# Eight batches of four places in the 32 rows of a column group, instead of four blocks of eight batches, in a two-layer recurrence

## The chip, the cores and the metric

The kernel runs on one core of one Trainium2 chip. The metric is the device time of one execution, in microseconds. Before the change the median of 3 runs is 2086.43 us (2085.79 to 2086.91).

## The reference

Two residual layers, each a plain tanh recurrence over 1024 positions, with 8 batches and 512 features, all in float32:

```python
# x: (8, 1024, 512), cond: (8, 512); Wx, Wh: (512, 512), b: (512,) of each layer
def layer(x, h0, Wx, Wh, b):
    xW = einsum('ntd,dh->tnh', x, Wx) + b
    def step(h, xw_t):
        h_next = tanh(h @ Wh + xw_t)
        return h_next, h_next
    _, hs = scan(step, h0, xW)
    return swapaxes(hs, 0, 1)

x = x + layer(x, cond, L0_Wx, L0_Wh, L0_b)
x = x + layer(x, cond, L1_Wx, L1_Wh, L1_b)
```

A step of a layer needs all of the step before it. Layer 1 at position n needs layer 0's output at position n.

## The kernel before, in words

**Interleaving.** Layer 1 runs eight steps behind layer 0 (`LAG`). Slot s does step s of layer 0 and step s - 8 of layer 1, so there are 1032 slots: in the first eight only layer 0 works, in the last eight only layer 1. In between are 1016 slots with two steps each. In the text below, a step of one layer is "a step", and "the other layer" is the one whose step lies before or after it.

**Column groups.** TensorE is used as four column groups of 32 columns. The weights it holds (the stationary operand) are 32 columns of h or x, and the moving operand is a 128x128 piece of Wh or Wx. Group g produces 32 rows of PSUM (partitions 32g to 32g+31) that hold features 128g to 128g+127 of the output. A k tile is one fourth of the 512 features that are summed over; for it, h has 32 columns of float32 next to each other, and these 32 columns become the 32 rows of every group. Eight batches fill only 8 of the 32 columns. The other 24 are three more *places* for the same eight batches.

**What the places hold.** Before the change, place t of a tile is the block of columns 8t to 8t+7. For the projection x @ Wx, the four places are four successive positions, so that one pass over Wx serves four steps. For step n of the recurrence, the h of step n is put into place (n+1) % 4. For the k tiles 2 and 3 the other places stay zero, and they are multiplied as float32 (`recur_whole`, line 236). For the k tiles 0 and 1, h is cut into bfloat16 parts: the first part is the upper half of h itself, the second is the upper half of h minus the first part, and the third the upper half of what remains then. The second and third part go to two neighbouring places (table `BLOCKS`), and the weights are also in three bfloat16 parts (`recur_parts`, line 253: 2 tiles x 3 parts x 4 groups = 24 matmuls). The rows of PSUM at three neighbouring places then hold terms of one sum, and the fourth place holds nothing.

**One step on the engines.** ACT first writes the projection of the step into the PSUM bank, with the rows of the other positions set to zero by a mask (`begin`, line 339). TensorE adds `recur_whole` and `recur_parts`. Then:

1. `turn` (DVE, line 418) transposes the 128x128 of PSUM in 32x32 blocks into `zt` in SBUF. In it, the 32 columns of a tile k are what the 32 rows were.
2. `total` (DVE, line 424) adds three places of `zt` (from `LOWEST[n % 4]` on) into `z`: 96 elements of each partition become 32.
3. `tanh` (ACT, line 344) writes 32 elements into the place of h.
4. `rest_first` (DVE, line 432) subtracts from h (tiles 0 and 1, 16 elements) its upper half and writes the difference to the next place; `rest_second` (same line) does it once more.
5. `sum_mid` (line 458) or `sum_out` (line 468) adds h to x, 32 elements, on DVE.

**Order.** Every engine works its queue in program order; there is no planner. On TensorE (`slot`, line 272) each slot is: parts of layer 0, a tile of projection, whole of layer 1, parts of layer 1, a tile of projection, whole of layer 0's next step. `recur_whole` waits for `tanh` of the step before, `recur_parts` for its `rest_second`. On DVE (`slot`, line 481) a slot is: `turn(0)`, `rest_second(1)`, `total(0)`, the sums, `rest_first(0)`, `turn(1)`, `rest_second(0)`, `total(1)`, `rest_first(1)`. So `turn` of one layer stands in the queue behind `rest_first` of the other, and ahead of its `rest_second`. `rest_first` waits for the `tanh` of its step, `total` for its `turn`, `tanh` for its `total`. x is loaded and the result stored by four positions at a time (64 KB), on SP's queue.

**What the change touches.** `window` (149), `h_of` (156), `h_cols` (165), `x_of` (171), `total` (420), `rest` (429), the masks (line 506) and the order of x in DRAM. `turn`, `project`, `recur_whole` and `recur_parts` are untouched: each reads 32 columns of a tile.

Of the kernel before, what the change touches and what calls it, by code (L numbers as in the profile page):

```python
# [12 lines left out]
P = 128  # L13
B, T, D = 8, 1024, 512
KC = D // P
KB = (2, 2)
PARTS = 3
QG = 4
S4 = 4
ROWS = S4 * B  # L20
COLS = KC * B
GRP = S4 * COLS
# [4 lines left out]
HALF = 4 * (P + B)  # L27
# [9 lines left out]
def number(l, s):  # L37
    n = s - LAG * l
    return n if 0 <= n < T else None
# [6 lines left out]
PROJECT = (((0, 1), (0, 2)), ((0, 3), (1, 0)), ((1, 1), (1, 2)), ((1, 3), (0, 0)))  # L46


BLOCKS = ((0, 1, 2), (1, 0, 2), (2, 1, 3), (3, 1, 2))
LOWEST = (0, 0, 1, 1)  # L50


def build(nc, x, h_init, weights, out):
    ctx = ExitStack()
    with ctx:
        def sb(name, shape, dt=F32):
            return ctx.enter_context(nc.sbuf_tensor(name, shape, dt))
# [4 lines left out]
        def sem(name):  # L62
            return ctx.enter_context(nc.semaphore(name))
# [11 lines left out]
        ones = sb("ones", [P, P])  # L75
# [5 lines left out]
        zt = [[sb(f"zt{l}_{i}", [P, P]) for i in range(2)] for l in LAYERS]  # L81
# [15 lines left out]
        s_ones = sem("ones_made")  # L97
# [32 lines left out]
        def h_count(l, n):  # L130

            s = n + LAG * l
            steps = [(m, t) for t in range(s - s % S4, s + 1) for m in LAYERS if counted(m, t)]
            return h_done[s // S4 % 2], steps.index((l, s)) + 1

        def is_split(l, n):

            return (n >= -S4 if l else n >= PARTED - 1) and n < T - 1

        def split_count(l, n):  # L140

            s = n + LAG * l
            return split_done[l][s // S4 % 2], s % S4 + 1
# [3 lines left out]
        def window(n):  # L147

            w = n % RING
            return w // 4 * HALF + w % 4 * P + (32 if w % 4 == 3 else 0), B * ((n + 1) % 4)  # L150

        def h_step(l, n):
            at, _ = window(n)
            return h[l][:, at:at + P].rearrange("p (k r) -> p k r", r=ROWS)

        def h_of(l, n):
            off = window(n)[1]
            return h_step(l, n)[:, :, off:off + B]

        def h_bits(l, n):  # L160

            at, _ = window(n)
            return h[l][:, at:at + P].bitcast(BF16).rearrange("p (k r two) -> p k r two", r=ROWS, two=2)[:, :, :, 1]

        def h_cols(n, part):


            at = BLOCKS[(n + 1) % S4][part] * B
            return slice(at, at + B)

        def x_of(xs, n):
            return xs[n // S4 % 2][:, :].rearrange("p (k s b) -> p s k b", s=S4, b=B)[:, n % S4]

        @block.sync
        def _(sp):
# [152 lines left out]
        def _(act):  # L328
# [13 lines left out]
            def tanh(l, n):  # L342
                act.wait_ge(z_done[l], n + 1)  # L343
                act.activation(h_of(l, n), z[l][n % 2][:, :].rearrange("p (k b) -> p k b", k=KC), ACT.Tanh).then_inc(  # L344
                    h_count(l, n)[0], 1)
# [68 lines left out]
        @block.vector  # L414
        def _(dve):
            def turn(l, n):
                dve.wait_ge(rec_done, STEP_AT[l, n])  # L417
                dve.transpose(zt[l][n % 2][:, :], ps_rec[l][n % 2][:, 0:P]).then_inc(zt_done[l], 1)  # L418

            def total(l, n):  # L420

                at = LOWEST[n % S4] * B
                dve.wait_ge(zt_done[l], n + 1)
                dve.tensor_reduce(z[l][n % 2][:, :].rearrange("p (k b) -> p k b", k=KC),  # L424
                                  zt[l][n % 2][:, :].rearrange("p (k r) -> p k r", r=ROWS)[
                                      :, :, at:at + PARTS * B].rearrange("p k (i b) -> p k b i", b=B),
                                  AX.X, ALU.add).then_inc(z_done[l], 1)

            def rest(l, n, part):

                step, to, of, tiles = h_step(l, n), h_cols(n, part), h_cols(n, part - 1), slice(0, KB[l])
                return dve.tensor_tensor(step[:, tiles, to], step[:, tiles, of], h_bits(l, n)[:, tiles, of],  # L432
                                         ALU.subtract)

            def rest_first(l, n):
                if is_split(l, n):
                    dve.wait_ge(*h_count(l, n))
                    rest(l, n, 1).then_inc(rest_done[l], 1)

            def rest_second(l, n):  # L440
                if is_split(l, n):
                    dve.wait_ge(rest_done[l], n + 1 if l else n + 2 - PARTED)
                    rest(l, n, 2).then_inc(split_count(l, n)[0], S4 if (l, n) == (0, PARTED - 1) else 1)

            def lower(l, n):

                if (n + LAG * l) % S4 == 0 and is_split(l, n - 1):
                    done, count = split_count(l, n - 1)
                    dve.sem_inc(done, -count)

            def sum_mid(n):

                c, t = n // S4, n % S4
                if n >= 2 * S4:
                    dve.wait_ge(out_done, n - 2 * S4 + 1)
                if n == T - 1:
                    dve.wait_ge(*h_count(0, n))
                add = dve.tensor_tensor(x_of(x_mid, n), x_of(x_dve, n), h_of(0, n), ALU.add)  # L458
                if t == S4 - 1:
                    add.then_inc(mid_done, 1)  # L460

            def sum_out(n):
                c, t = n // S4, n % S4
                if t == 0 and c >= 2:
                    dve.wait_ge(out_free[c % 2], DMA * (c // 2))
                if n == T - 1:
                    dve.wait_ge(*h_count(1, n))
                dve.tensor_tensor(x_of(x_out, n), x_of(x_mid, n), h_of(1, n), ALU.add).then_inc(out_done, 1)  # L468

            def sums(s):  # L470

                c = (s + S4 - 1) // S4
                if s % S4 == 0 and c < NG:
                    dve.wait_ge(x_dve_loaded[c % 2], DMA * (c // 2 + 1))
                if (n := number(1, s - 1)) is not None:
                    sum_out(n)
                if (n := number(0, s - 1)) is not None:
                    sum_mid(n)

            def slot(s):  # L480

                n0, n1, before = number(0, s), number(1, s), number(1, s - 1)
                if n0 is not None:
                    turn(0, n0)
                if before is not None:
                    rest_second(1, before)
                if n0 is not None:
                    lower(0, n0)
                    total(0, n0)
                sums(s)  # L490
                if n0 is not None:
                    rest_first(0, n0)
                if n1 is not None:
                    turn(1, n1)
                if n0 is not None:
                    rest_second(0, n0)
                if n1 is not None:
                    lower(1, n1)
                    total(1, n1)
                    rest_first(1, n1)  # L500

            dve.memset(zeros[:, :], 0.0).then_inc(s_zeros, 1)
            dve.memset(h[0][:, :], 0.0).then_inc(s_clear, 1)
            dve.memset(ones[:, :], 0.0).then_inc(s_ones, 1)
            dve.wait_ge(s_ones, 1)
            for t in range(S4):
                at = (ROWS + B) * t
                dve.memset(ones[:, at:at + B], 1.0).then_inc(s_ones, 1)
            dve.wait_ge(s_ones, 1 + S4)
            dve.transpose(mask[:, :], ones[:, :]).then_inc(s_mask, 1)  # L510
            dve.wait_ge(s_clear, 2)
            dve.wait_ge(s_first, DMA)
            for dst in (h_of(0, -1), h_of(1, -1)):
                dve.tensor_copy(dst, h_first[:, :].rearrange("p (k b) -> p k b", k=KC)).then_inc(s_hinit, 1)  # L514
            dve.wait_ge(s_hinit, 2)
            rest(1, -1, 1).then_inc(s_hrest, 1)
            dve.wait_ge(s_hrest, 1)
            rest(1, -1, 2).then_inc(split_count(1, -1)[0], S4)
            for s in range(T + LAG + 1):
                slot(s)  # L520
# [28 lines left out]
```

## Time and profile before

| | |
|---|---|
| median of 3 runs | 2086.43 us |
| the profiled execution | 2085.73 us |
| its span | 2083.9 us |
| granted TensorE clock | 1.00 of full |
| busy, share of the span | PE 99%, weight loads 86%, DVE 82%, ACT 54%, POOL 1% |
| mean HBM traffic | 26 GB/s |

The profile is of one execution. Busy is the share of the span in which an engine had an instruction under way. Matmuls overlap and their ends are modelled, so the 99% of PE isn't a measure of how much it could still take. Weight loads (PEld) stand apart from the matmuls (PE), with which they overlap. "Idle before" is the time in which the engine had nothing under way before an instruction, with what released it. Instructions on DVE and ACT overlap a little too: one is started while the last one still writes.

### The profile page before, as it was taken

To read this page: it belongs to the slowest core of one execution; us is meant where nothing else is said; L and a number is where in the kernel's file an instruction comes from. 1 tells how busy PE (TensorE), PEld (TensorE's weight loads), DVE (VectorE), ACT (ScalarE), POOL (GpSimd) and SP (SyncE) were. 2 spreads that over 40 slices of the span, in tenths; PEclk is the share of its full clock that TensorE was granted. 3 is DMA by queue.
4 is the path that set the end of the run, shared out by engine and by line. 5 is a ranking of instruction groups with operands and counts; after the bars stand their busy time and mean duration, and the time that the engine had idled before them with its cause. 6 is when DMAs were issued, how large, how long until landed. Compare 5 with 4: busy or idle time off the path is not lost.

```text
span 2083.9 us, 213827 instructions
## 1 busy us (share of the span) xinstructions
PE 2065.8 (99%) x98428; PEld 1792.3 (86%) x98428; DVE 1716.2 (82%) x10234; ACT 1121.8 (54%) x4612; POOL 14.3 (1%) x22
## 2 busy tenths in 40 slices
PE   7999999999999999999999999999999999999998
PEld 6888888888888888888888888888888888888887
DVE  5888888888888888888888888888888888888887
ACT  3555555555555555555555555555555555555554
POOL 2000000000000000000000000000000000000000
PEclk9999999999999999999999999999999999999999
DMA  3000000000000000000000000000000000000000
GB/s 107 23 27 23 27 23 27 23 27 23 27 23 27 23 27 23 27 23 27 23 27 23 27 23 27 23 27 23 27 23 27 23 27 23 27 23 27 23 27 15
DMA packets 112495, 56.00 MB, mean 27 GB/s; under 512 B 12496, under 2 KB 111072, under 8 KB 112096
## 3 DMA queue, kind: packets, MB, share of 16 engines
q1 hardware_dynamic: 111456, 53.53, 9.0%
q14 instruction: 130, 1.06, 0.2%
q10 hardware_dynamic: 864, 1.18, 0.2%
q8 instruction: 13, 0.21, 0.0%
q0 software_dynamic: 32, 0.02, 0.0%
HBM read 37.90 MB, written 16.78 MB: 26 GB/s over the span
## 4 chain that ended last, share of the span: by engine, by line
PE 98%; DVE 0%; DMA 0%; issue 0%; ACT 0%; SPq 0%; DVEq 0%; ACTq 0%
PE ps_rec L236 43%; PE ps_rec L253 34%; PE ps_xw L215 21%; DMA wh<-wh_in 0%; DVE zt L418 0%; DVE z L424 0%; ACT h L344 0%; SPq L181 0%; SPq L183 0%; SPq L179 0%; ACT ps_rec L339 0%; DVE x_out L468 0%; DVEq L417 0%; ACTq L343 0%
## 5 line engine op out<-in xcount | busy, mean ns | idle before, releaser
L236 PE MATMUL ps_rec<-wh,h 128*32 128x128 f32 x32912 | 1256.3, 273 | 11.2 <-ACT h L344 8.4
L253 PE MATMUL ps_rec<-wh_part,h 128*32 128x128 bf16 x48960 | 1058.8, 221 | 2.3 <-issue 2.3
L344 ACT ACTIVATE h<-z 128x32 f32<-128x32 f32 x2048 | 470.2, 230 | 826.0 <-DVE z L424 809.9
L236 PEld LDWEIGHTS ps_rec<-wh,h 128*32 128x32 f32 x32912 | 826.8, 109 | 89.3 <-ACT h L344 13.8
L432 DVE TENSOR_TENSOR h<-h 128x16 f32<-128x16 f32 x4080 | 627.0, 154 | 303.2 <-ACT h L344 302.7
L253 PEld LDWEIGHTS ps_rec<-wh_part,h 128*32 128x32 bf16 x48960 | 705.4, 96 | 193.9 <-issue 2.8
L339 ACT ACTIVATE ps_rec<-ps_xw,mask 128x128 f32<-128x128 f32 x2048 | 670.5, 328 | 119.4 <-PE ps_xw L215 94.8
L418 DVE STREAM_TRANSPOSE zt<-ps_rec 128x128 f32<-128x128 f32 x2048 | 638.8, 312 | 19.9 <-PE ps_rec L236 10.8
L424 DVE TENSOR_REDUCE z<-zt 128x32 f32<-128x96 f32 x2048 | 544.2, 266 | 1.5 <-DVE zt L418 0.9
L215 PE MATMUL ps_xw<-wx,x_pe 128*32 128x128 f32 x8232 | 402.7, 273 | 0.3 <-DMA wx<-wx_in 0.3
L215 PE MATMUL ps_xw<-wx,x_mid 128*32 128x128 f32 x8192 | 401.4, 273 | 0.0
L458 DVE TENSOR_TENSOR x_mid<-x_dve,h 128x32 f32<-128x32 f32 x1024 | 198.1, 193 | 35.1
L468 DVE TENSOR_TENSOR x_out<-x_mid,h 128x32 f32<-128x32 f32 x1024 | 185.4, 181 | 0.3 <-ACT h L344 0.3
L215 PEld LDWEIGHTS ps_xw<-wx,x_pe 128*32 128x32 f32 x8232 | 181.7, 110 | 1.3 <-DMA wx<-wx_in 0.8
L215 PEld LDWEIGHTS ps_xw<-wx,x_mid 128*32 128x32 f32 x8192 | 181.0, 110 | 0.0
L332 ACT ACTIVATE ps_xw<-bias 128x128 f32<-128x128 f32 x514 | 142.0, 277 | 10.2 <-DMA bias<-b_in 2.1
L300 PE MATMUL ps_rec<-zeros 128*32 128x512 bf16 x100 | 8.3, 465 | 0.0
L300 PEld LDWEIGHTS ps_rec<-zeros 128*32 128x32 bf16 x100 | 3.1, 118 | 2.6 <-issue 2.2
L408 POOL TENSOR_TENSOR wh_rest<-wh 128x512 f32<-128x512 f32 x4 | 4.1, 1037 | 6.8 <-DMA wh<-wh_in 6.7
L412 POOL TENSOR_TENSOR wh_part<-wh_rest 128x512 bf16<-128x512 f32 x4 | 4.1, 1036 | 0.0
L514 DVE COPY h<-h_first 128x32 f32<-128x32 f32 x2 | 0.3, 176 | 4.5 <-DMA h_first<-cond_t 4.5
L386 ACT ACT_TABLE_LOAD x1 | 1.3, 1283 | 4.2 <-issue 4.2
(18 smaller groups left out, 11.1 us busy)
## 6 DMA issues: line engine op xcount, KB each, us to landing
x_pe<-x_t SPq DMA_DIRECT2D x256, 64.0 KB, 1.8
x_dve<-x_t SPq DMA_DIRECT2D x256, 64.0 KB, 1.9
out_t<-x_out SPq DMA_DIRECT2D x256, 64.0 KB, 1.5
wh<-wh_in SPq DMA_DIRECT2D x1, 1024.0 KB, 4.7
wx<-wx_in SPq DMA_DIRECT2D x1, 1024.0 KB, 8.1
wx<-wx_in ACTq DMA_DIRECT2D x2, 256.0 KB, 5.5
wx<-wx_in SPq DMA_DIRECT2D x2, 256.0 KB, 5.3
wh<-wh_in SPq DMA_DIRECT2D x2, 256.0 KB, 7.3
```

Of the source, the lines that this page charges most:

```text
L215: mm = pe.matmul(rows(ps_xw[l][c % 2], g), src, wx[l][:, k, g * P:(g + 1) * P], start=False, stop=False, skip_group_check=True, tile_posit ...
L236: mm = pe.matmul(rows(ps_rec[l][n % 2], g), h_step(l, n - 1)[:, k, :], wh[l][:, k, g * P:(g + 1) * P], start=False, stop=k == KC - 1 and n ...
L253: mm = pe.matmul(rows(ps_rec[l][n % 2], g), h_bits(l, n - 1)[:, k, :], wh_part[l][:, i, at:at + P], start=False, stop=k == KB[l] - 1 and i ...
L300: pe.matmul(bank[32 * g:32 * g + 32, :], zeros[:, 0:ROWS], zeros[:, :], start=True, stop=False, skip_group_check=True, tile_position=(0, 3 ...
L332: return act.activation(ps_xw[l][c % 2][:, 0:P], bias[l][:, :], ACT.Copy)
L339: act.activation(ps_rec[l][n % 2][:, 0:P], ps_xw[l][c % 2][:, 0:P], ACT.Copy, scale=mask[:, 32 * t:32 * t + 1]).then_inc(begun[l], 1)
L344: act.activation(h_of(l, n), z[l][n % 2][:, :].rearrange("p (k b) -> p k b", k=KC), ACT.Tanh).then_inc(h_count(l, n)[0], 1)
L418: dve.transpose(zt[l][n % 2][:, :], ps_rec[l][n % 2][:, 0:P]).then_inc(zt_done[l], 1)
L424: dve.tensor_reduce(z[l][n % 2][:, :].rearrange("p (k b) -> p k b", k=KC), zt[l][n % 2][:, :].rearrange("p (k r) -> p k r", r=ROWS)[:, :, ...
L432: return dve.tensor_tensor(step[:, tiles, to], step[:, tiles, of], h_bits(l, n)[:, tiles, of], ALU.subtract)
L458: add = dve.tensor_tensor(x_of(x_mid, n), x_of(x_dve, n), h_of(0, n), ALU.add)
L468: dve.tensor_tensor(x_of(x_out, n), x_of(x_mid, n), h_of(1, n), ALU.add).then_inc(out_done, 1)
```

## The change

The place becomes the inner index of a tile's 32 columns, and the batch the outer one: place t of batch b is column 4b + t instead of 8t + b. The kernel's arithmetic, the number of instructions and their order stay. The addresses change: `total` reads three places that are neighbours in memory, and goes on to the next batch 4 floats further, where it read three elements 8 floats apart. `tanh`, `rest`, `sum_mid` and `sum_out` touch one float in four, where they had runs of eight. x is stored in DRAM with the position innermost, and a load is still one contiguous row of each partition. `BLOCKS` is renamed to `PLACES`.

```diff
-BLOCKS = ((0, 1, 2), (1, 0, 2), (2, 1, 3), (3, 1, 2))
+PLACES = ((0, 1, 2), (1, 0, 2), (2, 1, 3), (3, 1, 2))
 LOWEST = (0, 0, 1, 1)
...
-            return w // 4 * HALF + w % 4 * P + (32 if w % 4 == 3 else 0), B * ((n + 1) % 4)
+            return w // 4 * HALF + w % 4 * P + (32 if w % 4 == 3 else 0), (n + 1) % 4
...
         def h_of(l, n):
-            off = window(n)[1]
-            return h_step(l, n)[:, :, off:off + B]
+            return h_step(l, n).rearrange("p k (b s) -> p k b s", s=S4)[:, :, :, window(n)[1]]
...
-        def h_cols(n, part):
-            at = BLOCKS[(n + 1) % S4][part] * B
-            return slice(at, at + B)
+        def place(ap, n, part):
+            return ap.rearrange("p k (b s) -> p k b s", s=S4)[:, :, :, PLACES[(n + 1) % S4][part]]
 
         def x_of(xs, n):
-            return xs[n // S4 % 2][:, :].rearrange("p (k s b) -> p s k b", s=S4, b=B)[:, n % S4]
+            return xs[n // S4 % 2][:, :].rearrange("p (k b s) -> p s k b", s=S4, b=B)[:, n % S4]
...
             def total(l, n):
-                at = LOWEST[n % S4] * B
+                at = LOWEST[n % S4]
                 dve.wait_ge(zt_done[l], n + 1)
                 dve.tensor_reduce(z[l][n % 2][:, :].rearrange("p (k b) -> p k b", k=KC),
-                                  zt[l][n % 2][:, :].rearrange("p (k r) -> p k r", r=ROWS)[
-                                      :, :, at:at + PARTS * B].rearrange("p k (i b) -> p k b i", b=B),
+                                  zt[l][n % 2][:, :].rearrange("p (k b s) -> p k b s", b=B, s=S4)[
+                                      :, :, :, at:at + PARTS],
                                   AX.X, ALU.add).then_inc(z_done[l], 1)
 
             def rest(l, n, part):
-                step, to, of, tiles = h_step(l, n), h_cols(n, part), h_cols(n, part - 1), slice(0, KB[l])
-                return dve.tensor_tensor(step[:, tiles, to], step[:, tiles, of], h_bits(l, n)[:, tiles, of],
+                step, bits = h_step(l, n)[:, 0:KB[l], :], h_bits(l, n)[:, 0:KB[l], :]
+                return dve.tensor_tensor(place(step, n, part), place(step, n, part - 1), place(bits, n, part - 1),
                                          ALU.subtract)
...
             for t in range(S4):
-                at = (ROWS + B) * t
-                dve.memset(ones[:, at:at + B], 1.0).then_inc(s_ones, 1)
+                dve.memset(ones[:, t * ROWS:(t + 1) * ROWS].rearrange("p (b s) -> p b s", s=S4)[:, :, t],
+                           1.0).then_inc(s_ones, 1)
```

The host code orders x and the result in the same way.

## Rows read from the trace of the kernel before

**Rows 1.** The page: busy time and share of each engine.
```profile
PE 2065.8 (99%) x98428; PEld 1792.3 (86%) x98428; DVE 1716.2 (82%) x10234; ACT 1121.8 (54%) x4612; POOL 14.3 (1%) x22
```

**Rows 2.** Timeline, two steps: start us, us, engine, line, instruction [idle <-releaser].
```profile
1002.15 0.17 DVE L432 TENSOR_TENSOR h<-h 128x16 f32<-128x16 f32 x1
1002.17 0.40 PEld L236 LDWEIGHTS ps_rec<-wh,h 128*32 128x32 f32 x16
1002.23 0.61 PE L236 MATMUL ps_rec<-wh,h 128*32 128x128 f32 x16
1002.25 0.31 DVE L418 STREAM_TRANSPOSE zt<-ps_rec 128x128 f32<-128x128 f32 x1
1002.48 0.13 DVE L432 TENSOR_TENSOR h<-h 128x16 f32<-128x16 f32 x1
1002.59 0.26 DVE L424 TENSOR_REDUCE z<-zt 128x32 f32<-128x96 f32 x1
1002.66 0.34 PEld L253 LDWEIGHTS ps_rec<-wh_part,h 128*32 128x32 bf16 x24
1002.67 0.52 PE L253 MATMUL ps_rec<-wh_part,h 128*32 128x128 bf16 x24
1002.89 0.23 ACT L344 ACTIVATE h<-z 128x32 f32<-128x32 f32 x1 [0.33 <-DVE z L424]
1003.15 0.17 DVE L432 TENSOR_TENSOR h<-h 128x16 f32<-128x16 f32 x1 [0.30 <-ACT h L344]
1003.24 0.31 DVE L418 STREAM_TRANSPOSE zt<-ps_rec 128x128 f32<-128x128 f32 x1
```

**Rows 3.** Timeline, the last eight steps, layer 1 alone.
```profile
2072.48 0.52 PE L253 MATMUL ps_rec<-wh_part,h 128*32 128x128 bf16 x24
2073.04 0.32 DVE L418 STREAM_TRANSPOSE zt<-ps_rec 128x128 f32<-128x128 f32 x1 [0.56 <-PE ps_rec L253]
```

**Rows 4.** Groups by line, 500 to 1500 us: count | busy us, mean ns | idle before.
```profile
L253 PEld LDWEIGHTS ps_rec<-wh_part,h 128*32 128x32 bf16 x23976 | 344.9, 96 | 94.0
L418 DVE STREAM_TRANSPOSE zt<-ps_rec 128x128 f32<-128x128 f32 x1000 | 311.8, 312 | 0.0
L432 DVE TENSOR_TENSOR h<-h 128x16 f32<-128x16 f32 x1999 | 306.9, 154 | 147.7 <-ACT h L344 147.7
L424 DVE TENSOR_REDUCE z<-zt 128x32 f32<-128x96 f32 x999 | 265.7, 266 | 0.4 <-DVE zt L418 0.4
L344 ACT ACTIVATE h<-z 128x32 f32<-128x32 f32 x999 | 229.4, 230 | 391.9 <-DVE z L424 383.9
L215 PEld LDWEIGHTS ps_xw<-wx,x_pe 128*32 128x32 f32 x4000 | 88.0, 110 | 0.0
```

**Rows 5.** Line 253, 1002 to 1003 us: ns min/median/max.
```profile
L253 PE MATMUL ps_rec<-wh_part,h x40: 219/219/228, 1001.8 to 1003.0; 128*32 128x128 bf16 x40
```

**Rows 6.** Lines 432 (one `rest_first`, from 1002.15), 458, 514, 386: ns min/median/max.
```profile
L432 DVE TENSOR_TENSOR h<-h x1: 175/175/175, 1002.2 to 1002.2; 128x16 f32<-128x16 f32 x1
...
L458 DVE TENSOR_TENSOR x_mid<-x_dve,h x499: 191/192/195, 501.5 to 1498.5; 128x32 f32<-128x32 f32 x167
...
L514 DVE COPY h<-h_first x2: 173/176/180, 7.5 to 7.6; 128x32 f32<-128x32 f32 x2
...
L386 ACT ACTIVATE table<-zeros x1: 203/203/203, 5.5 to 5.5; 128x1 f32<-128x1 bf16 x1
```

**Rows 7.** Line 418, whole span: the number of steps.
```profile
L418 DVE STREAM_TRANSPOSE zt<-ps_rec x2048: 306/311/319, 11.2 to 2080.8; 128x128 f32<-128x128 f32 x187
```

More of the change, by code:

```diff
@@ L530 @@
     arrays = {
-        "x_t": packed(x.reshape(B, T // S4, S4, QG, KC, 32).transpose(3, 5, 1, 4, 2, 0).reshape(P, T // S4, GRP)),
+        "x_t": packed(x.reshape(B, T // S4, S4, QG, KC, 32).transpose(3, 5, 1, 4, 0, 2).reshape(P, T // S4, GRP)),
         "cond_t": packed(cond.reshape(B, QG, KC, 32).transpose(1, 3, 2, 0).reshape(P, COLS)),
@@ L547 @@
     return np.ascontiguousarray(
-        got.reshape(QG, 32, T // S4, KC, S4, B).transpose(5, 2, 4, 0, 3, 1).reshape(B, T, D))
+        got.reshape(QG, 32, T // S4, KC, B, S4).transpose(4, 2, 5, 0, 3, 1).reshape(B, T, D))
```

## The prediction

> **What bounds the kernel now.** The page comes first [rows 1]: PE is busy for 99% of the span, weight loads for 86%, DVE for 82%, ACT for 54%. That looks like a TensorE kernel, and the change gives TensorE not one instruction more or less. But PE's ends are modelled, so the next view is the timeline of two steps in the middle [rows 2], read for who starts right after whom. One step takes 1.00 us there (`turn` starts at 1002.25 and 1003.24; 1000 transposes in 1000 us [rows 4]). Every start has a predecessor that it follows as closely as it can, and these close into loops:
>
> - **Loop A, on DVE and ACT.** `turn` starts at 1002.25, `total` 0.34 later (0.31 of transpose and 0.03 of semaphore), `tanh` 0.30 later (0.26 and 0.03 to 0.04), `rest_first` 0.26 later (0.23 and 0.03), and the other layer's `turn`, which stands behind it in DVE's queue, 0.09 later. The sum, 0.99 to 1.00, is the whole period. ACT had been idle when `tanh` began, for `total`, and DVE when `rest_first` began, for `tanh` (147.7 us over 1000 steps [rows 4]); neither is waiting for TensorE.
> - **Loop B, through TensorE.** `turn` 1002.25, `rest_second` of the other layer behind it at 1002.48, the first weight load of that layer's parts at 1002.66 (0.13 of work and 0.05 of semaphore), the matmuls at 1002.67, and the next `turn` at 1003.24, 0.57 after them. This too sums to 1.00.
> - **TensorE itself.** Its loads of the parts come 0.01 us ahead of their matmuls, while those of `recur_whole` come 0.06 ahead [rows 2], and the load engine idles 94 ns a step before the parts and not at all before the projection [rows 4]. The parts' loads are thus late: the first matmuls of the parts take 228 ns instead of 219 [rows 5]. So PE's own need is about 9 ns under the period, some 991 ns.
>
> Is `turn` held by TensorE or by `rest_first`? In the last eight steps DVE is idle before `turn`, and it starts 0.56 us after the parts' matmuls did [rows 3]. In the middle it is 0.57 [rows 2]. So `turn` could start about 0.01 us earlier for all that TensorE holds it back, and loop A is the tightest, with loop B and TensorE within about 10 ns (1%) of it. That is the frame of the forecast: nothing shorter than about 10 ns a step can be won, and every ns added to loop A is paid in full, 2032 times. That number is the 2048 steps [rows 7] less 16, the eight of each layer that run alone.
>
> **The change part by part.** The sum goes by ns a step.
>
> *`total`*, in loop A. It reads 96 elements, now 8 floats apart and then three neighbours. What has the stride cost so far? Started from idle, `rest_first` takes 175 ns for 16 elements and `sum_mid` 192 for 32 [rows 6], which is 1.06 ns an element on 158 ns fixed. By this, 96 elements without any stride cost would take 158 + 102 = 260 ns, and `total` takes 266 [rows 4]. So I take -6. The other end: against the copy, which writes the same 32 elements and reads 32 instead of 96 in 176 ns [rows 6], the 64 more cost 1.41 ns each; if all above half of that were stride, 96 x 0.4 = 37 ns would go. The end on the other side is 0; runs of three that start at an odd float might even cost, but the strided form has no such run to compare, and I leave it at 0.
>
> *`rest_first`*, in loop A by the time it keeps DVE (`turn` starts 0.09 after it), and *`rest_second`*, in loop B by its full length. Both read two operands and write one, all with one float in four; now they have runs of eight. No row shows an operation with scattered writes. The low end is 0. For the high end I let each of the 16 elements cost as much as three contiguous ones: 2 x 16 x 1.06 = +34. I take +17, one more element time for each element: half-way, and a guess, since the nearest row, the contiguous 1.06 ns, says only what such an element costs at least.
>
> The Trainium skill, "Vector Engine (DVE) Microarchitecture Reference", section 5.2, says that a port runs at full rate only while its elements come in pairs of adjacent 4-byte words, and gives 1.05 ns a column for contiguous operands, 1.98 when all three hop at every element and about 2.50 for a small step. Going by it alone, 16 elements would cost 15 to 23 ns more, an estimate from that page; no run here shows it yet.
>
> *`tanh`*, in loop A by its full length. It reads `z` as before, contiguous, and writes one float in four. One element takes 203 ns and 32 take 230 [rows 6, 4], 0.84 ns an element. The low end is 0, the high end one more element time each, 32 x 0.84 = +27. I take +5: only one of its two sides is scattered, and 0.84 ns an element is ACT's reckoning of its own rate, not of the memory's.
>
> *The sums*, with 32 scattered elements on three operands: +34 at the value taken for `rest`. `sum_mid` or `sum_out` ends well before the next `rest_first`, which finds DVE idle for 0.30 us [rows 2]. With the cover of 300 ns they cost nothing. *TensorE*: the same 32 adjacent columns per load, nothing. *Loads and stores*: the same contiguous rows, nothing. *Masks*: four small writes at the start, under 0.1 us.
>
> Loop A: -6 + 17 + 5 = +16 ns. Loop B: -10 of slack, +17 = +7; it stays beneath, and TensorE gets slack. 2032 x 16 ns = +32.5 us. In the eight steps at the end, where one layer is alone, both rests are in the chain: 8 x (34 - 6 + 5) = +0.3 us; in the first eight there are no parts and it is nothing. The profiled execution took 2085.73 us, so 2085.7 + 32.8 = 2118.5; the median of the runs lies 0.7 us above that execution, so **2119 us**, 1.6% slower.
>
> **The rivals.**
>
> - *R1, scattering is free.* 16 or 32 elements are few, and the extra time could hide in the fixed 158 ns. For it: 96 strided reads in `total` show almost no cost. Against it: those are reads of one operand with one write for three reads, while `rest` has two reads and a write for every element. Then only `total` changes, by -6 to -37. Loop A falls by that, and TensorE and loop B stop the gain at about -10. At -6 it is 2086.4 - 12 = 2074, at -10 2066 us.
> - *R2, it cancels, or the period isn't loop A's.* If `total` gives back as much as `rest` and `tanh` take, within 2 ns, or if a step has more room than I read from starts printed to 10 ns, the time stays at 2086.4. Against it: the four intervals of loop A add up to the period with nothing left over.
> - *R3, loop B takes over.* If strides in `total` did cost (-37) and `rest` costs +17, loop A is 1000 - 37 + 17 + 5 = 985, but `rest_second` is in loop B: 1000 - 10 + 17 = 1007. That is 2086.4 + 14 = 2101 us, slower although `total` became much faster. The point from which it decides: as soon as `rest_second` grows by over 10 ns, no gain in `total` can make the kernel faster. The same section of the Trainium skill gives 1.73 ns an element where one source hops at every element, by which `total` would have been paying a good 60 ns for its stride (an estimate from the page); its 266 ns speak against that.
> - *R4, scattering is dear.* `rest` at +34, `tanh` at +10, `total` -5: +39 a step, 2086.4 + 79 + 0.5 = 2166 us.
>
> That the change doesn't do what it says has little room: `total` will read three neighbours, and all other patterns are plain in the diff.
>
> **How the numbers follow.** Forecast 0.42, with its own range 2103 to 2143 (+8 to +28 ns a step); R1 0.23; R2 0.13; R3 0.10; R4 0.12. Faster and slower mean by over 0.2%, about 4 us or 2 ns a step, which is what measurements of this kernel can tell from none. Faster is R1, 0.23; same is R2, 0.13; slower is the rest, 0.64. The range goes from R1's lower end to the cheap side of R4: 2066 to 2152.
>
> **What would show it.** Durations in the changed profile: line 424 at about 260 ns instead of 266; line 432 from 175 to about 192 for `rest_first`, and `rest_second` from 0.13 us to about 0.15; line 344 from 230 to about 235; lines 458 and 468 some 30 ns longer. The distance from `rest_first` to `turn` from 0.09 to 0.11, the period 1.016, and the weight loads of the parts further ahead of their matmuls than 0.01, since TensorE now waits a little. Idle of PE or PEld before line 236 or 253 should appear. I am wrong if `rest` keeps its durations, if `total` falls by more than 10 ns, or if the period doesn't move although loop A's parts do.

## The result

The changed kernel takes 2155.69 us (median of 6 runs, 2154.54 to 2157.03) against 2086.91 us of the kernel before (6 runs beside them): 1.0331 times as long, 95% interval 1.032 to 1.0342. That is 3.3% or 68.8 us slower. Slower was forecast, but 1.6% of it, and the time lies above the range given (2066 to 2152).

The timeline of the changed kernel, two steps from the middle; the lines answer to [rows 2], with line 430 for 432, 416 for 418, 422 for 424 and 342 for 344:

```profile
1001.78 0.19 DVE L430 TENSOR_TENSOR h<-h 128x16 f32<-128x16 f32 x1
1001.89 0.31 DVE L416 STREAM_TRANSPOSE zt<-ps_rec 128x128 f32<-128x128 f32 x1
1002.12 0.15 DVE L430 TENSOR_TENSOR h<-h 128x16 f32<-128x16 f32 x1
1002.23 0.25 DVE L422 TENSOR_REDUCE z<-zt 128x32 f32<-128x96 f32 x1
1002.33 0.34 PEld L251 LDWEIGHTS ps_rec<-wh_part,h 128*32 128x32 bf16 x24
1002.33 0.52 PE L251 MATMUL ps_rec<-wh_part,h 128*32 128x128 bf16 x24
1002.52 0.26 ACT L342 ACTIVATE h<-z 128x32 f32<-128x32 f32 x1 [0.29 <-DVE z L422]
1002.81 0.20 DVE L430 TENSOR_TENSOR h<-h 128x16 f32<-128x16 f32 x1 [0.33 <-ACT h L342]
1002.91 0.31 DVE L416 STREAM_TRANSPOSE zt<-ps_rec 128x128 f32<-128x128 f32 x1
```

The instructions of both loops follow one another as closely as before. `turn` starts at 1001.89 and 1002.91, 1.02 apart in this pair; over the middle it is 967 steps in 1000 us. The groups by line of the same stretch, 500 to 1500 us, against [rows 4 and 6] (count | busy us, mean ns | idle before):

```profile
L430 DVE TENSOR_TENSOR h<-h 128x16 f32<-128x16 f32 x1932 | 331.9, 172 | 159.5 <-ACT h L342 159.5
L416 DVE STREAM_TRANSPOSE zt<-ps_rec 128x128 f32<-128x128 f32 x967 | 298.2, 308 | 0.0
L342 ACT ACTIVATE h<-z 128x32 f32<-128x32 f32 x966 | 255.6, 265 | 400.0 <-DVE z L422 391.7
L422 DVE TENSOR_REDUCE z<-zt 128x32 f32<-128x96 f32 x966 | 244.4, 253 | 0.4 <-issue 0.4
L456 DVE TENSOR_TENSOR x_mid<-x_dve,h 128x32 f32<-128x32 f32 x483 | 109.0, 226 | 16.5
L466 DVE TENSOR_TENSOR x_out<-x_mid,h 128x32 f32<-128x32 f32 x483 | 104.2, 216 | 0.1
```

Means of single durations: `total` won 13 ns (266 to 253), the rests lost 18 (154 to 172), the sums 34 each, and `tanh` 35 (230 to 265). The page of the changed kernel has a warning for whoever reads busy shares. Its first row and the first of its chain of waits, and behind them the chain's row of the kernel before:

```profile
PE 2135.4 (99%) x98428; PEld 1783.4 (83%) x98428; DVE 1751.0 (81%) x10234; ACT 1140.4 (53%) x4612; POOL 14.4 (1%) x22
...
DVE 80%; ACT 13%; issue 5%; PE 2%; DMA 0%; SPq 0%; DVEq 0%; ACTq 0%
```
```profile
PE 98%; DVE 0%; DMA 0%; issue 0%; ACT 0%; SPq 0%; DVEq 0%; ACTq 0%
```

PE is "99% busy" in both, with the same 98428 matmuls, and took 70 us more of it: with matmuls that overlap and ends that are modelled, waiting looks like work. The chain went through PE before and goes through DVE and ACT now.

Of the signs that the prediction named, those on durations are answered above. The idle time of the load engine before the parts rose from 94 to 128 ns a step, but PE shows none, and the parts' loads did not move further ahead of their matmuls: by the starts in the trace they are 3 ns ahead before the change and 2 ns after it. The loads still follow `rest_second` at once: they come 202.5 ns after its start, of which 150 are its own time, and came 185.7 after it with 132 before the change.

The timeline prints hundredths of a us, and a step's sum needs less. So the loops are followed below in means of the distances between starts, in ns, worked out from the starts in the trace between 200 and 1900 us (1640 to 1720 steps for each). Loop A is `turn` to `total` to `tanh` to `rest_first` to the other layer's `turn`; loop B is `turn` to `rest_second` to the first load of the parts to the next `turn`.

```
kernel               period | A: turn-total  -tanh  -rest_first  -turn | B: turn-rest_second  -loads  -turn
before               1000.9 |     346.7      299.2     262.2      92.8 |        236.1         185.7   578.9
after                1035.1 |     343.5      286.7     297.6     107.3 |        232.8         202.5   599.8
e1 total only        1000.4 |     351.4      286.8     262.7      99.6 |        240.5         185.7   574.1
e2 tanh only         1031.4 |     344.1      297.7     297.0      92.5 |        233.1         185.8   612.5
e3 rests only        1020.0 |     350.5      296.2     262.5     110.7 |        239.7         205.2   575.1
e4 sums only         1001.4 |     347.7      296.8     266.8      90.1 |        236.3         186.0   579.1
e5 after, tanh back  1017.7 |     351.0      286.5     266.6     113.7 |        240.2         202.4   575.1
e6 rest_first only   1012.0 |     343.6      298.0     262.6     107.8 |        233.0         185.3   593.6
e7 rest_second only  1018.8 |     351.1      295.4     262.6     109.7 |        240.4         204.0   574.4
e8 pairs             1002.4 |     350.1      289.3     267.5      95.5 |        239.2         187.2   576.0
e11 no rest_second    996.5 |     345.3      296.8     262.1      92.3 |          -             -       -
e12 same, and total   991.5 |     349.8      287.6     262.0      92.1 |          -             -       -
```

Both sums equal the period in every row (to 0.2 ns), since distances around a closed loop always do; that they add up says nothing about which loop decides. Which loop is the tight one is read from two columns: the last of A is 92 to 93 where `turn` only waits for DVE to get done with `rest_first` (107 to 108 where that is scattered), and more where it waits for TensorE; the last of B is 574 to 576 where `turn` waits for TensorE alone, and more where it doesn't.

### The profile page after: what moved, and what is told of

The parts are those of the page before. It is cut to its first block, busy times and chain, and to the rows that moved or that the text cites. A ratio compares the mean times of both kernels' runs of the same rounds, so it can differ in the third digit from the quotient of the medians.

```text
span 2153.3 us, 213827 instructions
## 1 busy us (share of the span) xinstructions
PE 2135.4 (99%) x98428; PEld 1783.4 (83%) x98428; DVE 1751.0 (81%) x10234; ACT 1140.4 (53%) x4612; POOL 14.4 (1%) x22
## 3 DMA queue, kind: packets, MB, share of 16 engines
q14 instruction: 130, 1.06, 0.2%
## 4 chain that ended last, share of the span: by engine, by line
DVE 80%; ACT 13%; issue 5%; PE 2%; DMA 0%; SPq 0%; DVEq 0%; ACTq 0%
DVE h L430 24%; DVE z L422 21%; DVE zt L416 17%; ACT h L342 13%; DVE x_mid L456 11%; DVE x_out L466 7%; PE ps_rec L234 1%; PE ps_rec L251 0%; DMA wh<-wh_in 0%; PE ps_xw L213 0%; SPq L179 0%; SPq L181 0%; SPq L177 0%; ACT ps_rec L337 0%; DVEq L415 0%
## 5 line engine op out<-in xcount | busy, mean ns | idle before, releaser
L342 ACT ACTIVATE h<-z 128x32 f32<-128x32 f32 x2048 | 541.7, 264 | 870.2 <-DVE z L422 852.8
L430 DVE TENSOR_TENSOR h<-h 128x16 f32<-128x16 f32 x4080 | 701.5, 172 | 338.6 <-ACT h L342 338.1
L234 PEld LDWEIGHTS ps_rec<-wh,h 128*32 128x32 f32 x32912 | 817.4, 109 | 99.5 <-ACT h L342 14.1
L416 DVE STREAM_TRANSPOSE zt<-ps_rec 128x128 f32<-128x128 f32 x2048 | 631.8, 309 | 19.5 <-PE ps_rec L234 11.3
L422 DVE TENSOR_REDUCE z<-zt 128x32 f32<-128x96 f32 x2048 | 518.3, 253 | 1.5 <-issue 0.6
L456 DVE TENSOR_TENSOR x_mid<-x_dve,h 128x32 f32<-128x32 f32 x1024 | 232.1, 227 | 34.8
L466 DVE TENSOR_TENSOR x_out<-x_mid,h 128x32 f32<-128x32 f32 x1024 | 220.6, 215 | 0.5 <-ACT h L342 0.3
```

What stands on the lines that cost most here:

```text
L234: mm = pe.matmul(rows(ps_rec[l][n % 2], g), h_step(l, n - 1)[:, k, :], wh[l][:, k, g * P:(g + 1) * P], start=False, stop=k == KC - 1 and n ...
L430: return dve.tensor_tensor(place(step, n, part), place(step, n, part - 1), place(bits, n, part - 1), ALU.subtract)
```

## The experiments

Each part of the change was made alone on the kernel before.

**e1: `total` only.** It adds the wrong places.

```diff
-                at = LOWEST[n % S4] * B
+                at = LOWEST[n % S4]
-                                  zt[...].rearrange("p (k r) -> p k r", r=ROWS)[:, :, at:at + PARTS * B].rearrange("p k (i b) -> p k b i", b=B),
+                                  zt[...].rearrange("p (k b s) -> p k b s", b=B, s=S4)[:, :, :, at:at + PARTS],
```

> The kernel before, with one part of the change alone: total reads three neighbouring floats and goes on by four (it adds the wrong terms; everything else stays in blocks). Theory (two loops): total takes 253 ns instead of 266, as in the changed kernel, so loop A falls from 1001 to about 985 ns a step, but loop B (turn, rest_second, loads of the parts, matmuls) and TensorE stop it at 991 to 996: 2067 to 2077 us. Rival 1 (only loop A counts): -16 ns a step in full, 2054 us. Rival 2 (TensorE alone sets the 1001 ns): no change, 2087 us.

2085.41 us against 2087.65, ratio 0.9989 (0.998 to 0.9999): next to nothing, where the theory had expected 2067 to 2077. `total` did take 253 ns, and its distance in loop A fell by 12. But B's last distance fell only to 574.1 and A's last rose to 99.6: `turn` now waited for TensorE. It also ran longer, as its mean in the groups by line shows (312 in [rows 4]):

```profile
L418 DVE STREAM_TRANSPOSE zt<-ps_rec 128x128 f32<-128x128 f32 x999 | 316.6, 317 | 0.0
L424 DVE TENSOR_REDUCE z<-zt 128x32 f32<-128x96 f32 x1000 | 253.2, 253 | 0.4 <-DVE zt L418 0.4
```

So loop B, when it is the tight one, comes to 1000 ns. It had no 10 ns to spare. This run alone doesn't yet tell loop B from TensorE's own need.

**e2: `tanh` only.** h holds its values in the wrong columns.

```diff
-                act.activation(h_of(l, n), z[l][n % 2]...
+                act.activation(scat(h_step(l, n), (n + 1) % S4), z[l][n % 2]...   # scat: one float in four
```

> The kernel before, with one part of the change alone: tanh writes one float in four (so h holds the values in the wrong columns; nothing else changes). Theory: tanh takes 264 instead of 230 ns and loop A grows by the whole of it, +35 ns a step x 2032 = +71 us, 2158 us, although TensorE and loop B have no more to do. Rival (the 35 ns come only because DVE scatters at the same time, the two getting in each other's way): tanh stays at 230 ns and the time at 2087 us. Rival (part of it was hidden in slack): 2120 us or less.

2147.29 us, ratio 1.0287 (1.027 to 1.0305), a little under the 2158 expected. `tanh` takes 264 ns without any scattered work on DVE, so it isn't contention:

```profile
L348 ACT ACTIVATE h<-z 128x32 f32<-128x32 f32 x970 | 256.5, 264 | 409.1 <-DVE z L428 397.8
L428 DVE TENSOR_REDUCE z<-zt 128x32 f32<-128x96 f32 x970 | 256.2, 264 | 0.5 <-DVE zt L422 0.5
```

The period grew by 30.5 rather than 35: `turn` and `total` are 3 and 1.5 ns quicker to pass on, `turn` because it now starts well after TensorE would let it (more on this at the end).

**e3: both rests only.** The rests work on a tile `hs` of their own, of h's shape.

```diff
-                return dve.tensor_tensor(step[:, tiles, to], step[:, tiles, of], h_bits(l, n)[:, tiles, of], ALU.subtract)
+                return dve.tensor_tensor(scat(step, to), scat(step, of), scat(bits, of), ALU.subtract)
```

> The kernel before, with one part of the change alone: rest_first and rest_second read and write one float in four (of a tile of their own that nobody else reads, so the parts 2 and 3 of h are missing). Theory: 175 to 193 and 131 to 149 ns; loop A grows by 15 to 18 ns a step, loop B by 18 from 10 below the period, so loop A decides: +30 to +37 us, 2117 to 2124 us. Rival (loop B has no slack, both rests are paid): +36 ns, 2160 us. Rival (rests hidden): 2087 us.

2124.22 us, ratio 1.0175 (1.0158 to 1.0192), at the upper end of what was expected, but not for the reason given: the table has A's last distance at 110.7 and B's at 575.1, so loop B decided here, at 1020. It had no 10 ns of slack, as the rival says, but the two rests aren't added up either.

**e4: the sums only.** `x_of` as in the changed kernel, and h from `hs`, a tile of zeros, one float in four.

> The kernel before, with one part of the change alone: sum_mid and sum_out read and write one float in four (h from a tile of its own that stays zero). Theory: both become 34 ns longer (192 to 226, 181 to 215) and the time stays within 0.1% of 2087 us, since DVE is idle for 300 ns behind them. Rival (DVE's total time matters, it is 82% busy): +17 ns a step on average or more, 2120 us.

2086.42 us, ratio 0.9994 (0.9984 to 1.0003): no change, with sums of 224 and 216 ns:

```profile
L471 DVE TENSOR_TENSOR x_mid<-x_dve,hs 128x32 f32<-128x32 f32 x499 | 112.0, 224 | 17.1
L481 DVE TENSOR_TENSOR x_out<-x_mid,hs 128x32 f32<-128x32 f32 x500 | 108.2, 216 | 0.0
```

The reason given doesn't hold, though. The 0.30 us of idle time that the expectation and the prediction count on stand before layer 1's `rest_first`. Both sums stand behind `total` of layer 0 and directly ahead of layer 0's `rest_first`. The last sum and that `rest_first`, in the kernel before (for the second see [rows 2], from 1002.15) and in e4:

```profile
1001.99 0.19 DVE L458 TENSOR_TENSOR x_mid<-x_dve,h 128x32 f32<-128x32 f32 x1
```
```profile
1001.71 0.22 DVE L471 TENSOR_TENSOR x_mid<-x_dve,hs 128x32 f32<-128x32 f32 x1
1001.84 0.17 DVE L445 TENSOR_TENSOR h<-h 128x16 f32<-128x16 f32 x1
```

Between 200 and 1900 us, `rest_first` started 29 ns before the end of `sum_mid` in the kernel before and 87 ns before it in e4. One DVE instruction starts at most 76 to 89 ns before the end of the one ahead in these traces, so the cover was some 60 ns, an estimate from these numbers, and not 300. The two sums added 34 + 34 = 68, and in layer 0 `rest_first` came 271 ns after the start of `tanh` instead of 262. The time doesn't show it: `total` took 263 ns instead of 266 here, `rest_first` of layer 0 only 170 instead of 175, and the mean period is 1001.4 against 1000.9. In the changed kernel the longer `tanh` pays for the cover: `rest_first` starts 60 ns before the end of `sum_mid`, as `tanh` demands. With `tanh` put back (e5) it is 89 ns again, and 271 ns after `tanh`.

**e5: the changed kernel with `tanh` put back.**

```diff
-                act.activation(h_of(l, n), z[l][n % 2]...
+                act.activation(h_step(l, n)[:, :, B * window(n)[1]:B * window(n)[1] + B], z[l][n % 2]...
```

> The changed kernel, with tanh alone put back to runs of eight floats (so h holds its values in the wrong columns). Theory (two loops): tanh 264 -> 230 ns; loop A falls by 35 from 1035 to 1000 ns a step, and now loop B decides, with rest_second at 150 ns: about 240 + 203 + 575 = 1018, so 2120 to 2125 us, half of what the tanh is worth by itself. Rival (a single loop, each part's cost is simply added): 1000 ns, 2084 to 2087 us.

2119.76 us, ratio 1.0158 (1.0141 to 1.0175), just under the range expected. `tanh` alone costs 60 us on the kernel before (e2) and gives back only 36 here. This is the strongest sign of two loops: with a single one the two numbers would be nearly equal.

**e6 and e7: one rest at a time.**

```diff
+                if part == 1:      # e6; e7: part == 2
+                    return dve.tensor_tensor(scat(step, to), scat(step, of), scat(bits, of), ALU.subtract)
```

> The kernel before, rest_first alone with one float in four (both rests on a tile of their own that nobody reads; parts 2 and 3 of h are missing). Theory: rest_first is in loop A only, by the time it holds DVE, +15 ns, and T's own time may give 3 of it back: a period of 1012 to 1016 ns, 2110 to 2118 us; loop B unchanged near 1000. Rival (all of e3's +19 ns came through loop B): no change, 2087 us.

> The kernel before, rest_second alone with one float in four (both rests on a tile of their own). Theory: rest_second is in loop B only, 132 -> 150 ns; e1 showed that loop B has nothing to spare, and so all of it is paid: 1018 to 1020 ns, 2121 to 2125 us, as e3 with both rests. What the prediction had said (10 ns of slack in loop B): 1008 ns, 2102 us. Rival (all of e3 came through loop A): 2087 us.

e6: 2107.89 us, ratio 1.0102 (1.0085 to 1.0119), 2 us under the range expected, a period of 1012.0, all through loop A (107.8 and 593.6 in the last columns). e7: 2121.77 us, ratio 1.0169 (1.0152 to 1.0186), 1018.8, all through loop B (574.4), and as much as both together in e3. The two add 15 and 18 ns to different loops, and the longer loop counts. In e7 `turn` is at 317 ns again:

```profile
L431 DVE STREAM_TRANSPOSE zt<-ps_rec 128x128 f32<-128x128 f32 x982 | 310.9, 317 | 0.0
L449 DVE TENSOR_TENSOR hs<-hs 128x16 f32<-128x16 f32 x982 | 172.2, 175 | 145.2 <-ACT h L357 145.2
L447 DVE TENSOR_TENSOR hs<-hs 128x16 f32<-128x16 f32 x981 | 147.7, 151 | 0.0
```

**e8: pairs of batches.** Column 8c + 2s + d of a tile holds place s of batch 2c + d, in h, PSUM and x.

```diff
+        def place_of(ap, at):
+            return ap.rearrange("p k (c s d) -> p k c s d", s=S4, d=2)[:, :, :, at, :]
...
+                dve.tensor_reduce(z[l][n % 2][:, :].rearrange("p (c d) -> p c d", d=2),
+                                  zt[l][n % 2][:, :].rearrange("p (c s d) -> p c d s", d=2, s=S4)[:, :, :, at:at + PARTS],
```

> A layout between the two, with the reference's result: the 32 columns are four pairs of batches, each with its four places, so column 8c + 2s + d. tanh, rest and the sums touch runs of two adjacent floats, total reads three floats 2 apart. Theory (an operand costs extra only where an element has no adjacent neighbour): tanh 230, rest 175 and 132, sums 192 and 182 as in blocks, total 253 to 266, period 1000: 2085 to 2088 us. Rival (cost follows the number of runs, or any stride): half of the changed kernel's extra times or more, tanh 247 and rest 184, 2120 us or above.

2088.61 us, ratio 1.001 (1.0 to 1.002), 0.6 us above the range expected. Runs of two floats cost almost nothing, and `total`, whose three floats now lie two apart, keeps most of its gain:

```profile
L434 DVE TENSOR_TENSOR h<-h 128x16 f32<-128x16 f32 x1996 | 309.7, 155 | 150.1 <-ACT h L346 150.1
L426 DVE TENSOR_REDUCE z<-zt 128x32 f32<-128x96 f32 x998 | 255.2, 256 | 0.4 <-DVE zt L420 0.4
L346 ACT ACTIVATE h<-z 128x32 f32<-128x32 f32 x997 | 233.9, 235 | 390.3 <-DVE z L426 383.2
```

The time doesn't follow, as in e1: loop B decides (576.0), and nothing in it became shorter.

**e9: which side of a rest costs.** Layer 0 (line 450) scatters the result, layer 1 (line 452) the two sources; the other side is in runs.

> The kernel before, with the rests on tiles of their own (parts 2 and 3 of h are missing): in layer 0 only the result is written one float in four and both sources are runs, in layer 1 only the two sources are read one float in four and the result is a run. Which side costs the 18 ns of 16 elements? Theory W (writes without an adjacent neighbour cost, reads don't, as total's reads hardly did): layer 0 193 and 150 ns, layer 1 175 and 132. Rival R (reads cost): the other way round. Rival (either side alone costs nearly all, and they overlap): both near 190 and 148.

```profile
L452 DVE TENSOR_TENSOR ht<-hs 128x16 f32<-128x16 f32 x985 | 166.8, 169 | 145.7 <-ACT h L358 145.7
L450 DVE TENSOR_TENSOR ht<-hs 128x16 f32<-128x16 f32 x985 | 165.8, 168 | 0.0
```

These are means over both rests of a layer, against 154 with runs on all sides and 172 with none. (The second source, the upper halves of floats, is every second 2-byte value even in a "run".) Either side alone costs 14 to 15 ns and both 18: the last rival is right, and theory W is wrong. The 2115.64 us of this single run aren't used.

**e10: `tanh` at other distances.** Into a tile of its own, layer 0 (line 359) every second float, layer 1 (line 362) every eighth.

> The kernel before, with tanh writing to a tile of its own (h stays as it was at the start): layer 0 every second float, layer 1 every eighth. Does the distance matter, or only that there is no adjacent neighbour? Theory (a write of a float without its neighbour costs one more element time, whatever the distance): both 264 ns, as with every fourth, and with runs of two 235 (e8). Rival (the cost grows with the distance, or sets in only from 16 bytes on): layer 0 near 235, layer 1 at 264 or more.

```profile
L362 ACT ACTIVATE hs<-z 128x32 f32<-128x32 f32 x492 | 129.4, 263 | 203.1 <-DVE z L441 203.1
L359 ACT ACTIVATE hs<-z 128x32 f32<-128x32 f32 x492 | 116.2, 236 | 197.2 <-DVE z L441 185.8
```

Every eighth costs what every fourth does (263 and 264), every second hardly anything (236 against 230). It isn't the missing neighbour that costs: the rival is right in its second form, the cost sets in somewhere between 8 and 16 bytes of step.

**e11 and e12: without `rest_second`.** The third part of h is left out; a semaphore increment stands in its place. e12 has `total` as in e1 besides.

```diff
-                    rest(l, n, 2).then_inc(split_count(l, n)[0], ...)
+                    dve.sem_inc(split_count(l, n)[0], ...)
```

> The kernel before without rest_second (the third part of h is left out; a semaphore increment of DVE stands in its place, so the loads of the parts wait for rest_first alone). This takes loop B away and leaves loop A and TensorE's own need. Theory (loop A is as long as the period, 347 + 299 + 262 + 93): 999 to 1001 ns, 2083 to 2087 us. Rival (loop B alone set the period, loop A's sum is only pulled along): down to TensorE's need, about 990 ns, 2064 us.

> As e11, and total reads neighbours as in e1. Now loop A is 985 to 988 ns and loop B is away, so what remains is TensorE's own need. Theory (e1's 13 ns were lost because loop B had no slack): the period falls to TensorE's need, about 990 ns, 2062 to 2068 us. Rival (TensorE itself needs the 1000 ns): 2085 us, no change, as e1.

e11: 2076.88 us, ratio 0.9957 (0.994 to 0.9973), below the 2083 to 2087 expected. Loop A, tight (92.3), is 996.5 by itself: `turn` and `total` are a little shorter than in [rows 4]. e12: 2066.20 us, ratio 0.9906 (0.989 to 0.9923), 991.5 a step. The `total` that was worth nothing in e1 is worth 5 ns here, and what TensorE needs is not above 991.5. So it was loop B that swallowed e1's gain, not TensorE.

**e13 to e15: `rest_second` on POOL**, after the same semaphore, in the kernel before (e13), with pairs (e14), and in the changed kernel (e15).

> The kernel before, with rest_second on POOL (GpSimd) instead of DVE, after the same semaphore; the reference's result. Theory: it no longer stands behind the other layer's transpose; it may take up to 280 ns on POOL before the parts' loads are as late as before, so loop B is away and loop A stays: 996 ns as e11, 2077 us. Rival (POOL is slow to start or the two engines hinder each other on SBUF, as sum_mid's 560 to 674 ns beside POOL's work at the start suggest): rest_second over 300 ns or DVE's operations longer, 2100 us or more.

> The layout of pairs (e8) with rest_second on POOL; the reference's result. Theory: loop A is 996 - 10 (total) + 5 (tanh) = 991 to 993 ns and TensorE's need 990: 2066 to 2070 us, faster than both kernels by 0.8 to 1.0%. Rival as in e13: 2095 us or more.

> The changed kernel with rest_second on POOL; the reference's result. Theory (in the changed kernel loop A alone sets the period, and rest_second is not in it): 1033 to 1036 ns, 2151 to 2157 us, no change against the changed kernel. Rival (rest_second's 18 ns are part of the loss): about 1017 ns, 2119 us.

e13: 2090.38 us, ratio 1.0016 (1.0006 to 1.0025). e14: 2088.88 us, 1.0008 (0.9999 to 1.0018). Neither gains. From the timeline of e13:

```profile
1001.65 0.18 DVE L177 TENSOR_TENSOR h<-h 128x16 f32<-128x16 f32 x1
1001.75 0.31 DVE L430 STREAM_TRANSPOSE zt<-ps_rec 128x128 f32<-128x128 f32 x1
1001.91 0.21 POOL L177 TENSOR_TENSOR h<-h 128x16 f32<-128x16 f32 x1 [0.81 <-DVE h L177]
1002.17 0.35 PEld L259 LDWEIGHTS ps_rec<-wh_part,h 128*32 128x32 bf16 x24
```

Lines of other engines are left out. POOL starts 0.08 us after `rest_first` ended and takes 0.21, and the loads come 0.52 after `rest_first` began; on DVE it was 0.51 (1002.15 to 1002.66 in [rows 2]). What waiting behind the transpose costs on DVE, POOL loses by starting late and running long. DVE's operations beside it did not get longer (`turn` 313, `rest_first` 175).

e15: 2158.13 us, ratio 1.0339 (1.0321 to 1.0356), against 1.0331 for the changed kernel with `rest_second` on DVE: no difference to speak of, though 1 us above the range expected. `rest_second` is not in the loop that sets the changed kernel's period; loop A is.

## Why the prediction was wrong

**Right:** that it gets slower, and by what mechanism. Busy shares aside, the changed kernel's period is a loop through DVE and ACT: its last distance is 107 ns, as in e6 where `turn` waits for the scattered `rest_first` alone, and e5 and e15 show that `tanh` counts in it and `rest_second` doesn't. (1035.1 - 1000.9) x 2032 = 69.5 us, where 68.8 were measured. Of R3's point the experiments confirm that a longer `rest_second` is paid although `total` gains: alone in e7, and together with the shorter `total` in e5. The sums cost nothing, as forecast, but by luck: the 300 ns of cover were read at the other layer's `rest_first`, and the real cover is some 60 ns (e4).

**The step that failed is the term for `tanh`: +5 ns a step taken, +35 measured.** The terms of loop A, in ns a step, the measured ones as differences of the first two rows of the table:

```
                          taken    bounds     measured
total                      -6     -37 to 0     -12.5
rest_first (time on DVE)  +17       0 to +34   +14.5
tanh                       +5       0 to +27   +35.4
turn                        0          -        -3.2
sum                       +16                  +34.2
```

`rest` was sized well: 175 to 194 and 132 to 150. The estimate of 15 to 23 ns that was worked out for it from the Trainium skill, "Vector Engine (DVE) Microarchitecture Reference", section 5.2, agrees with the 18 measured. `tanh` was taken at +5 because only one of its sides is scattered and because 0.84 ns an element was thought to be ACT's own pace. No row stood behind either reason, and e10 shows the first to be wrong: the write pattern alone moves `tanh` from 236 to 263 ns. The measured 35 / 32 = 1.1 ns for each float, on top of 0.84, is even above the bound, which allowed no more than one further element time *of ACT*. Per float it is the same 1.1 as on DVE (18 / 16), whose pace in a run the prediction read as 1.06. So DVE's element time would have been the better unit here; whether both engines pay for the same thing isn't shown. Had `tanh` been priced like `rest`, at 1.06 x 32 = +34, the sum would have been +45, 2178 us; and with the measured -13 for `total`, 2164 us.

**`total`** gained twice what was taken, within its bounds, and more than the 10 ns that the prediction had set as a sign of being wrong. (The lower bound is loosely worked: half of 1.41 over the 64 further elements is 45 ns, and 96 x 0.4 is 38, not 37.) Strides of 8 floats cost the reduction 13 ns in 266 (before against e1), 10 in 263 (e11 against e12). That is 0.1 ns an element and not the 0.7 more that the Trainium skill, "Vector Engine (DVE) Microarchitecture Reference", section 5.2, gives with its 1.73 ns for one hopping source of a two-source operation. The doubt that R3 raised about the 60 ns was right.

**The frame was off by some ns too, without effect on the time.** The prediction gave loop B 10 ns of slack and took loop A for the tightest. e1 and e7 show that loop B comes to 1000 when it is the tight one, and e11 that loop A by itself is 996.5. The slack was read from one difference of 0.01 us between starts printed to 0.01 us. B's last distance is 579.0 in the kernel before and 574 where TensorE alone holds `turn`, so 5 ns were left on average; and it left out that `turn` takes 317 ns instead of 312 when it starts straight behind TensorE, which uses these 5 up. The estimate of TensorE's need, 991 ns, fits e12: 991.5, with `turn` at 314 ns instead of e11's 309, where loop A without that would come to some 987 (996.5 less 10 for `total`, an estimate). The run doesn't show that the need isn't lower.

R4 came nearest in time (2166) with the wrong distribution: `rest` at +34 and `tanh` at +10. R1 (scattering is free) fails with e2 and e3. R2 (nothing changes) fails with e2, e6 and e7, where each added cost is paid, most of it or all; the room in a step that it speaks of is there only for savings (e1, e8). What stays open is why `turn` takes longer close behind TensorE, and why `total` over the same strides takes 266 ns in some kernels (before, e13) and 262 to 265 in others (e2 to e4, e6, e7, e11). e2 fell 11 us short of its expectation by these two together.

## What to carry to other kernels

Before an axis is moved inward for one instruction, list who writes and reads the same tile: here one reader gained 13 ns, and one writer in the same chain lost 35. Runs of two floats kept nearly all of both sides' speed (e8), so the choice isn't only between one and eight. And with two loops of one length, a saving in one is worth nothing (e1) and a cost in either is worth nearly all (30 of 35 ns in e2, 11 of 15 in e6, 18 of 18 in e7): find the second loop by taking an operation out (e11), before polishing the first (e1).

## What the runs showed of the hardware that was not expected

- ACT, 32 floats written: 230 ns in runs of eight, 235 in runs of two (e8), 236 to every second float, 264 to every fourth, 263 to every eighth (e10, e2). In the fast patterns each float written has the next one no more than 8 bytes away on one side, in the slow ones 16 bytes or more on both. Steps between 8 and 16 bytes were not tried.
- DVE, two sources, 16 elements: +14 with the result scattered, +15 with the sources, +18 with all (e9, e3). A reduction over 96 elements, whose scattered side is the one it reads: 262 to 266 ns at 8 floats' distance, 256 at 2, 253 adjacent.
- DVE's four memsets of 8 floats for the mask take 65 ns each, scattered one float in four as well as in a run (line 508 before, 505 after):

```profile
L505 DVE MEMSET ones<- x4: 65/65/65, 2.5 to 2.5; 128x8 f32 x4
```

- The transpose out of PSUM takes 317 ns where it follows TensorE at once (e1, e7) and 308 to 309 where it starts 19 ns or more later than that (after, e2, e6). The 312 of the kernel before is a mean over both: by B's last distance, read step by step from the trace between 200 and 1900 us, it takes 316 ns in the 328 steps below 576, 313 from 576 on, 310 from 579 on, and 309 in the 300 steps from 582 on.
